# First layer norm and value projection of an embedding tower made once per table row

## Chip, cores and metric

The kernel runs on one core of a Trainium2 chip. The metric is the device time of one execution in microseconds (us); lower is better. Engines: PE (TensorE, matrix products), DVE (VectorE), ACT (ScalarE), POOL (GpSimd), and SP, which issues DMAs. They run side by side, each in its own fixed order, and wait for one another through semaphores.

## What is computed

4096 tokens (8 batches of 512) are indices into a codebook of 2048 rows. All arithmetic is float32. Cut to what matters:

```
h = gelu(codebook[x] @ W1 + b1) @ W2 + b2                 # 256 columns per token
n = layernorm(h)                                          # (h - mean) / sqrt(var + 1e-5)
x_tok, x_pos = n[:, :128], n[:, 128:]
q, k, v = rotate(x_pos @ Wq), x_pos @ Wk, x_tok @ Wv      # 16 heads of 64; k and v have 4 heads
att = q k^T / 8 + slope * (i - j), causal
e = exp(att - max(att));  att = e / (1 + sum(e))
h = h + (att @ v) @ Wo
h = h + (gelu(layernorm(h) @ U1 @ V1 + c1) @ U2) @ V2 + c2
```

h, n, x_tok, x_pos and v of a token hang on its codebook row alone, not on its place in the batch.

## The kernel before

It has two parts, one after the other, with a barrier between them.

**The table** (`token_table`). The first line of the network is made for all 2048 codebook rows, not per token, in NC = 4 chunks of 512 rows. A chunk has KH = 8 steps, so there are STEPS = 32. In step n PE makes `first_product(n)` (six products of 512 columns), ACT the gelu (`hid`, L243), DVE splits it into a high half `hid_hi` (L303) and a rest `hid_lo` (L305), and PE makes `second_product(n)` (twelve products of 256 columns) two steps later. Splitting into hi and lo and multiplying hi·hi, lo·hi and hi·lo is how the kernel keeps float32 accuracy all through. At the end of a chunk DVE adds b2 (`keep_rows`, L276, two halves) into `made`, and SP stores two halves of 256 rows of 1024 B to `token_table` in DRAM (L172). `keep_rows(i)` waits until the stores of chunk i-1 have landed. In its gaps DVE also makes the hi and lo halves of the other weights (`halves`, L314) and the rotated Wq (L317 to L341).

**The layer** (`layer`). POOL gathers a batch's 512 rows with four indirect DMAs of 128 rows (`gather`, L565) into `h`. Then 16 heads of each batch are 16 slots, s = 16 i + j for batch i and head j; each engine's order is written out by hand per slot. In slot s PE makes the scores of head s (L950, L951), DVE adds slope and mask and finds the extreme (`least_of`, L734), ACT exponentiates (L607), DVE inverts the sums (L741, L743), POOL multiplies (`normalize(s-1)`, L577). PE turns head s-2 (`turn`, ten transposes, L960), ACT moves it (L614), and PE makes the products with v for two heads in each even slot (`values`, L974). `first(s)` and `second(s)` say what else stands in slot s, and each engine walks both lists: q for the next pair of heads in even slots, k in slots 1, 5, 9 and 13; of the batch before, the output projection w in slots 3 to 6, the second norm transposed (y) in slot 10, u in 11, the gelu burst (f, g) in 12, d in 15.

The first norm and the values of batch i+1 stand inside batch i:

- POOL: `gather(i+1)` in slot 1, `root` (a power of -1/2, L571) in slot 3.
- DVE: `norm_front` (four BATCH_NORM_STATS2, L696, four aggregates, L700) after slot 3, `norm_back` (L708 to L723, writes `xn`) after slot 5.
- x in slot 7: four transposes of `xn` for the position half (in `first`), four for the token half (in `second`), L854. ACT takes the hi half of each (L634), DVE the lo half (L760).
- v in slots 10 and 11: twelve products with wv each batch, six per slot (L846), copied to `v_sb` by DVE (L765).

x, q, k, v and the second half of y share one PSUM bank (`a_bank`), each waiting until its forerunner has been read. For batch 0 the norm, x, k and q stand ahead of slot 0 (the opening), and v in slots 0 and 1.

## Time and profile before

| what | value |
|---|---|
| time, median of 3 runs | 1024.96 us (1024.83 to 1025.38) |
| the profiled execution's own time | 1025.75 us |
| its span, first to last instruction | 1023.9 us |
| PE busy | 883.8 us, 86% of the span |
| ACT busy | 700.5 us, 68% |
| DVE busy | 648.4 us, 63% |
| POOL busy | 630.8 us, 62% |
| mean granted PE clock | 0.963 of full |

The span is cut into stretches below. A slot's length is told from the start of its first exponential on ACT (the 128x512 one) to that of the next slot. Shares of busy time over the whole span mix stages that have different limits, so each stage is read by itself.

### The profile page before, as it was taken

The page shows a single profiled execution, that of the slowest core. Times are in us where ns is not written, and L with a number is a line of the kernel's source. Part 1 is how long each engine was busy: PE and PEld are TensorE (multiplying, and loading weights), DVE is VectorE, ACT ScalarE, POOL GpSimd, SP SyncE. Part 2 cuts the span into 40 slices and gives each one's busy share as a digit, 9 for nine tenths or more (in the row PEclk, how much of TensorE's full clock was granted, in tenths as well). Part 3 has the DMA queues.
Part 4 walks back from the last instruction along what each step waited for, and adds up shares of the span by engine and source line. Part 5 has one row for each costly group of instructions (what it writes and reads, how often), then busy time and mean ns, then how long its engine had stood idle before and what let it go on. Part 6 is the DMA issues. An engine that isn't in the chain of part 4 may idle for free.

```text
span 1023.9 us, 17066 instructions
## 1 busy us (share of the span) xinstructions
PE 883.8 (86%) x5616; PEld 681.8 (67%) x5616; DVE 648.4 (63%) x2000; ACT 700.5 (68%) x1564; POOL 630.8 (62%) x599
## 2 busy tenths in 40 slices
PE   6999369999888997899888979899889988998776
PEld 5898246768656775578657855686567765786563
DVE  4566377777837776476747784778457774667321
ACT  5332067996768777786788677867687777878713
POOL 6000249898747966586748774787569674868420
PEclk9999679999999999999999999999899999999997
DMA  9200100000000000000001000000000000000000
GB/s 259 49 21 21 42 21 1 2 12 12 1 1 21 22 1 1 12 30 1 1 1 43 1 1 1 27 16 1 1 21 22 1 1 1 22 1 1 1 21 21
DMA packets 13782, 18.89 MB, mean 18 GB/s; under 512 B 2320, under 2 KB 11696, under 8 KB 13696
## 3 DMA queue, kind: packets, MB, share of 16 engines
q1 hardware_dynamic: 11088, 10.62, 3.3%
q0 software_dynamic: 2608, 7.18, 2.7%
q8 instruction: 46, 0.75, 0.3%
q14 instruction: 40, 0.33, 0.1%
HBM read 11.51 MB, written 6.29 MB: 17 GB/s over the span
## 4 chain that ended last, share of the span: by engine, by line
PE 47%; DVE 15%; ACT 11%; issue 10%; POOL 5%; DMA 0%; DVEq 0%; POOLq 0%; ACTq 0%
PE ps L846 14%; PE ps L974 8%; PE ps L960 8%; ACT probs L607 6%; PE ps L950 5%; DVE probs L734 4%; PE ps L951 4%; PE ps L930 3%; POOL probs L577 3%; PE ps L924 2%; DVE q_both L751 2%; ACT turned_sb L614 2%; POOL h L565 1%; DVE xn L723 1%; PE ps L925 1%
## 5 line engine op out<-in xcount | busy, mean ns | idle before, releaser
L577 POOL TENSOR_SCALAR probs<-probs,recip 128x512 f32<-128x512 f32 (+3 forms) x512 | 546.2, 1084 | 220.7 <-DVE recip L743 220.3
L734 DVE CUSTOM_DVE_ANT_0 probs<-ps,causal,slope 128x512 f32<-128x512 f32 (+3 forms) x512 | 259.5, 547 | 62.4 <-PE ps L951 56.9
L607 ACT ACTIVATE probs<-probs,least 128x512 f32<-128x512 f32 (+3 forms) x512 | 282.0, 553 | 24.6 <-DVE least L734 20.1
L614 ACT ACTIVATE turned_sb<-ps 128x1280 f32<-128x1280 f32 x128 | 157.7, 1232 | 115.1 <-PE ps L960 114.9
L950 PE MATMUL ps<-k_hi,q_both 128*128 128x512 f32 (+3 forms) x512 | 185.5, 362 | 25.8 <-DVE least L734 23.0
L974 PE MATMUL ps<-turned_sb,v_sb 128*64 128x512 f32 (+3 forms) x1024 | 152.0, 438 | 23.1 <-ACT turned_sb L614 23.1
L960 PE MATMUL ps<-ident,probs 128*128 128x128 f32 x1280 | 167.1, 279 | 3.9 <-POOL probs L577 3.7
L951 PE MATMUL ps<-k_lo,q_both 128*128 128x512 f32 (+3 forms) x512 | 153.9, 326 | 0.0
L960 PEld LDWEIGHTS ps<-ident,probs 128*128 128x128 f32 x1280 | 148.8, 145 | 5.7 <-POOL probs L577 5.2
L974 PEld LDWEIGHTS ps<-turned_sb,v_sb 128*64 128x64 f32 x1024 | 73.1, 136 | 111.1 <-issue 96.5
L950 PEld LDWEIGHTS ps<-k_hi,q_both 128*128 128x128 f32 x512 | 98.0, 191 | 71.5 <-DVE least L734 47.7
L951 PEld LDWEIGHTS ps<-k_lo,q_both 128*128 128x128 f32 x512 | 98.6, 192 | 4.5
L607 ACT ACTIVATION_READ_ACCUMULATOR probs<-probs,least 128x1 f32 x512 | 96.2, 188 | 0.0
L624 ACT ACTIVATE q_both<-ps 64x512 fp32r<-64x512 f32 x128 | 75.4, 589 | 26.2 <-PE ps L846 24.7
L751 DVE TENSOR_TENSOR q_both<-ps,q_both 64x512 fp32r<-64x512 f32 x128 | 88.1, 689 | 7.8 <-ACT q_both L624 4.1
L846 PE MATMUL ps<-wo_hi,o_hi 128*128 128x256 f32 x224 | 62.6, 280 | 0.0
L846 PE MATMUL ps<-wo_lo,o_hi 128*128 128x256 f32 x224 | 62.6, 279 | 0.0
L846 PE MATMUL ps<-wo_hi,o_lo 128*128 128x256 f32 x224 | 62.5, 279 | 0.0
L243 ACT ACTIVATE hid<-ps,b_col 128x512 f32<-128x512 f32 x32 | 22.0, 688 | 57.0 <-PE ps L367 56.8
L792 DVE TENSOR_TENSOR o_lo<-ps,o_hi 128x512 fp32r<-128x512 f32 x64 | 44.2, 690 | 22.7 <-ACT o_hi L659 22.6
L783 DVE TENSOR_TENSOR y_lo<-ps,y_hi 128x512 fp32r<-128x512 f32 x8 | 5.5, 691 | 81.4 <-ACT y_hi L653 81.4
L580 POOL MEMSET minus_half<- 128x4 f32 x1 | 0.1, 101 | 90.5 <-POOLq L147 90.5
(163 smaller groups left out, 1515.1 us busy)
## 6 DMA issues: line engine op xcount, KB each, us to landing
out_dram<-h SPq DMA_DIRECT2D x7, 512.0 KB, 2.9
rows<-in_L_tok_codebook_dram SPq DMA_DIRECT2D x4, 512.0 KB, 8.5
token_table<-made SPq DMA_DIRECT2D x8, 256.0 KB, 2.3
w_f<-in_L_tok_W_dram SPq DMA_DIRECT2D x2, 512.0 KB, 6.4
w_f<-in_L_tok_W_dram SPq DMA_DIRECT2D x4, 256.0 KB, 8.4
wo_f<-in_L_attn_Wo_dram POOLq DMA_DIRECT2D x1, 1024.0 KB, 10.4
wq_f<-in_L_attn_Wq_dram POOLq DMA_DIRECT2D x1, 512.0 KB, 7.2
v_f<-in_L_ffn_V_dram POOLq DMA_DIRECT2D x2, 256.0 KB, 7.5
```

Of the source, the lines that this page charges most:

```text
L577: ins = pool.tensor_scalar(at, at, recip[:, s % P_RING, q:q + 1], None, ALU.mult)
L607: act.activation(at, at, ACT.Exp, bias=least[:, s % P_RING, q:q + 1], scale=-1.0, accum_out=sums[:, s % P_RING, q:q + 1]).then_inc(exped, 1)
L614: act.activation(turned_sb[:, s % 2, :], turn_ps, ACT.Copy).then_inc(moved, 1)
L624: act.activation(q_both[at, s % 4, :], a_of("q", n, 0)[at, :], ACT.Copy).then_inc(q_high, 1)
L734: dve.tensor_tensor_reduce(out=probs[:, s % P_RING, at], in0=bank(unit % 2)[:, UNIT_AT[q]:UNIT_AT[q] + P * (q + 1)], in1=causal[:, at], sc ...
L751: dve.tensor_tensor(q_both[to, s % 4, :], a_of("q", n, 0)[at, :], q_both[at, s % 4, :].bitcast(F32), ALU.subtract).then_inc(q_low, 1)
L792: dve.tensor_tensor(o_lo[:, p % O_RING, :], o_bank, o_hi[:, p % O_RING, :].bitcast(F32), ALU.subtract)\
L846: mm = pe.matmul(dst, w, x, start=n == 0, stop=n == len(parts) - 1)
L950: pe.matmul(dst, w, k_hi[:, slot, 0:P * (q + 1)], start=True, stop=False)
L951: mm = pe.matmul(dst, w, k_lo[:, slot, 0:P * (q + 1)], start=False, stop=True)
L960: mm = pe.transpose(turn_ps[:, K_AT[k] + P * (q - k):K_AT[k] + P * (q - k + 1)], probs[:, s % P_RING, Q_AT[q] + P * k:Q_AT[q] + P * (k + 1 ...
L974: mm = pe.matmul(o_bank[rows, P * k:T], v_sb[:, b % 2, k, n // REP, :], turned_sb[:, (s + e) % 2, K_AT[k]:K_AT[k] + T - P * k], start=k == ...
```

## The change

Each table row becomes ROW = 640 floats (2560 B): the embedding (256), the normed position half (128), and the values (256). The norm and the value projection are made in `token_table`, for 2048 rows instead of 4096 tokens. The layer gathers whole rows and takes the position half and v from them.

- In the table part, per chunk: DVE `norm_front` at step 2 of the next chunk and `norm_back` at step 4, POOL one power, PE `turn_tokens` (four transposes) at the end of step 5, ACT and DVE the hi and lo halves, PE `make_values` (twelve products of 256 columns) at the end of step 7, ACT two copies (`keep_values`). For the last chunk all of this stands behind step 31. The stores wait for `v_kept`, not `row_kept`.
- `hid_hi` is made by ACT, not DVE. The halves of the weights and the rotated Wq move by a few steps.
- In the layer: no first norm on DVE, no root for it on POOL, four transposes less and twelve products less per batch on PE, no `tok_hi`, `tok_lo`, no copy to `v_sb`.

```diff
-    table = nc.dram_tensor("token_table", (ROWS, DIM), F32, kind="Internal").ap()
+    table = nc.dram_tensor("token_table", (ROWS, ROW), F32, kind="Internal").ap()
...
-                    sp.wait_ge(row_kept, 2 * i + n + 1)
+                    sp.wait_ge(v_kept, 2 * i + n + 1)
...
-                                 made[:, 2 * n:2 * n + 2, :]).then_inc(stored, 16)
+                                 made[:, 2 * n:2 * n + 2, P:P + ROW]).then_inc(stored, 16)
...
+            def tok_highs(i):
+                act.wait_ge(tok_full, i + 1)
+                if i >= 1:
+                    act.wait_ge(v_full, 2 * i)
+                act.activation(tok_hi[:, :], ct_bank(0), ACT.Copy).then_inc(tok_high, 1)
+
+            def keep_values(i):
+                for n in range(2):
+                    act.wait_ge(v_full, 2 * i + n + 1)
+                    act.activation(made[:, 2 * n:2 * n + 2, 2 * P + DIM:P + ROW], ct_bank(1 - n).rearrange("p (t c) -> p t c", t=2),
+                                   ACT.Copy).then_inc(v_kept, 1)
...
+                act.activation(hid_hi[:, n % HID_RING, :], hid[:, n % 2, :], ACT.Copy).then_inc(hid_high, 1)
...
+                if i >= 1 and m == TURN_AT:
+                    tok_highs(i - 1)
+                if i >= 1 and m == VALUES_AT:
+                    keep_values(i - 1)
...
+            def norm_back(i):
+                dve.wait_ge(guess_done, i + 1)
...
+                if i >= 1:
+                    dve.wait_ge(tok_full, i)
+                for t in range(NT):
+                    halves_of = made[:, t, 0:2 * (P + DIM)].rearrange("p (a c) -> p a c", a=2)[:, :, 0:P]
+                    ins = dve.tensor_scalar(halves_of, made[:, t, P:P + DIM].rearrange("p (a c) -> p a c", a=2),
+                                            row_mv[:, t, 0:1], guess[:, t:t + 1], ALU.subtract, ALU.mult)
+                ins.then_inc(normed, 1)
...
-                dve.tensor_copy(hid_hi[:, n % HID_RING, :], hid[:, n % 2, :]).then_inc(hid_high, 1)
...
             keep_rows(NC - 1)
+            norm_front(NC - 1)
+            norm_back(NC - 1)
+            tok_lows(NC - 1)
...
+            def turn_tokens(i):
+                pe.wait_ge(normed, i + 1)
...
+            def make_values(i):
+                pe.wait_ge(tok_low, i + 1)
...
+                if KH <= n < STEPS and n % KH == TURN_AT:
+                    turn_tokens(n // KH - 1)
+                if KH <= n < STEPS and n % KH == VALUES_AT:
+                    make_values(n // KH - 1)
+            turn_tokens(NC - 1)
+            make_values(NC - 1)
...
-    if i + 1 < B and j == 7:
-        out.append(("x", i + 1, 1))
-    if i + 1 < B and j in (10, 11):
-        out.append(("v", i + 1, j - 10))
...
-                    pool.indirect_dma_start(out=h[:, b % 3, t, :], out_offset=None, in_=g["table"],
+                    pool.indirect_dma_start(out=token_rows[:, b % 3, t, :], out_offset=None, in_=g["table"],
...
-                if i + 1 < B and j == 3:
-                    root(("x", i + 1))
...
-                if i + 1 < B and j == 3:
-                    norm_front(("x", i + 1))
-                if i + 1 < B and j == 5:
-                    norm_back(("x", i + 1))
...
-                    pe.wait_ge(xn_done, norm_no["x", n])
-                    turn_rows(a_of("x", n, m), 1 - m).then_inc(x_full, 1)
...
+                    pe.wait_ge(rows_in, 16 * NT * (n + 1))
+                    turn_rows(a_of("x", n, m), pos[:, n % 3, :, :]).then_inc(x_full, 1)
```

PE's order in slot 10 of a batch, before: the scores' last unit, eight transposes of y (`xn`), six value products, the turn of head s-2.

```order
L951 MATMUL ps<-k_lo,q_both 128x256
L854 MATMUL ps<-ident,xn 128x128 x8
L846 MATMUL ps<-wv_hi,tok_hi 128x256
L846 MATMUL ps<-wv_hi,tok_lo 128x256
L846 MATMUL ps<-wv_lo,tok_hi 128x256
L846 MATMUL ps<-wv_hi,tok_hi 128x256
L846 MATMUL ps<-wv_hi,tok_lo 128x256
L846 MATMUL ps<-wv_lo,tok_hi 128x256
L960 MATMUL ps<-ident,probs 128x128 x10
L950 MATMUL ps<-k_hi,q_both 128x512
```

The same place after:

```order
L1016 MATMUL ps<-k_lo,q_both 128x256
L926 MATMUL ps<-ident,xn 128x128 x8
L1025 MATMUL ps<-ident,probs 128x128 x10
L1015 MATMUL ps<-k_hi,q_both 128x512
L1016 MATMUL ps<-k_lo,q_both 128x512
```

The six products are gone and the turn follows the transposes at once.

PE's order where the table ends and the layer begins, before: the last products of `second_product`, two branches, then the eight transposes of the opening.

```order
L382 MATMUL ps<-w_hi,hid_lo 128x256
L147 UNCONDITIONAL_BRANCH
L825 UNCONDITIONAL_BRANCH
L854 MATMUL ps<-ident,xn 128x128 x8
L846 MATMUL ps<-pos_hi,wk_hi 128x512
```

The same place after: four transposes of `made` and twelve value products follow the table's last product (the last five of the products, the two branches, four transposes of `token_rows` and k's products come behind these rows).

```order
L463 MATMUL ps<-w_hi,hid_lo 128x256
L473 MATMUL ps<-ident,made 128x128 x4
L482 MATMUL ps<-wv_hi,row_hi 128x256
L483 MATMUL ps<-wv_hi,row_lo 128x256
L484 MATMUL ps<-wv_lo,row_hi 128x256
L482 MATMUL ps<-wv_hi,row_hi 128x256
L483 MATMUL ps<-wv_hi,row_lo 128x256
L484 MATMUL ps<-wv_lo,row_hi 128x256
L482 MATMUL ps<-wv_hi,row_hi 128x256
```

These sixteen products and transposes moved ahead of the barrier.

DVE's order at the end of the table after; before, the two rows of `made` (L276) were its last there, and the norm (L696) stood behind the branch. `row_mv`, `row_var` and `row_guess` hold mean and variance, variance, and the power.

```order
L417 TENSOR_TENSOR wq_lo<-rot,wq_hi 128x1024
L316 TENSOR_TENSOR made<-ps,b_row 128x2x256 x2
L324 BN_STATS row_stats<-made 128x6 x4
L327 BN_AGGR row_mv<-row_stats 128x2 x4
L329 TENSOR_SCALAR row_var<-row_mv 128x4
L333 TENSOR_TENSOR row_tmp<-row_guess 128x4
L334 TENSOR_TENSOR row_tmp<-row_tmp,row_var 128x4
L335 TENSOR_SCALAR row_tmp<-row_tmp 128x4
L336 TENSOR_TENSOR row_guess<-row_guess,row_tmp 128x4
L341 TENSOR_SCALAR made<-made,row_mv,row_guess 128x2x128 x4
L347 TENSOR_TENSOR row_lo<-ps,row_hi 128x512
```

The norm of the last chunk now stands ahead of its stores, and the stores ahead of the barrier.

## Rows read from the trace of the kernel before

**Rows 1.** Busy time by stretch: us, then engines, PEclk, DMA share; table, then opening.

```profile
0.00:107.33 107.33, 97.51 (x608) 86.81 (x608) 62.11 (x113) 40.06 (x60) 15.88 (x30) 1.00 0.32 84
107.33:137.13 29.80, 9.32 (x28) 7.04 (x28) 11.72 (x34) 5.44 (x9) 5.35 (x6) 0.58 0.11 35
```

**Rows 2.** The same (PE, PEld, DVE, ACT, POOL), batch 2: slots 3, 4-6, 7, 8-9, 10-11, 12.

```profile
341.49:349.19 7.70, 7.63 (x53) 6.19 (x55) 5.40 (x23) 4.72 (x12) 7.70 (x9) 1.00 0.04 13
349.19:370.76 21.57, 21.53 (x166) 18.55 (x162) 15.17 (x49) 13.96 (x33) 15.89 (x15) 1.00 0.00 1
370.76:377.19 6.43, 5.54 (x37) 3.94 (x39) 4.77 (x20) 5.10 (x13) 2.99 (x4) 1.00 0.00 0
377.19:387.42 10.23, 9.06 (x60) 6.47 (x58) 9.86 (x33) 8.97 (x23) 9.38 (x10) 1.00 0.01 2
387.42:404.22 16.80, 13.24 (x81) 10.80 (x79) 11.26 (x33) 10.40 (x24) 12.21 (x11) 0.90 0.00 0
404.22:420.62 16.40, 14.45 (x78) 8.30 (x75) 5.18 (x16) 12.84 (x22) 4.39 (x5) 1.00 0.01 1
```

**Rows 3.** The same six stretches of slots in the last batch (batch 7).

```profile
887.06:894.49 7.43, 7.41 (x53) 6.17 (x55) 4.04 (x16) 4.72 (x12) 6.80 (x7) 1.00 0.01 2
894.49:915.49 21.00, 20.58 (x160) 17.88 (x156) 11.56 (x37) 13.45 (x32) 11.18 (x12) 1.00 0.00 1
915.49:920.12 4.63, 4.41 (x27) 3.35 (x29) 4.53 (x22) 4.58 (x11) 4.05 (x5) 1.00 0.00 0
920.12:930.04 9.92, 9.19 (x63) 6.79 (x60) 9.32 (x33) 9.07 (x22) 8.75 (x9) 1.00 0.01 2
930.04:944.66 14.62, 12.36 (x73) 9.69 (x71) 10.68 (x31) 10.41 (x25) 13.72 (x13) 0.88 0.00 1
944.66:960.25 15.59, 12.89 (x67) 7.07 (x64) 4.31 (x13) 12.24 (x21) 2.10 (x2) 1.00 0.00 1
```

**Rows 4.** Timeline of PE in slot 10 of batch 2: start, length, [idle before <-who ended it].

```profile
392.65 0.58 PE L846 MATMUL ps<-wv_hi,tok_hi 128*128 128x256 f32 x1 [2.31 <-DVE y_lo L776]
```

**Rows 5.** Busy time by stretch, batch 0: slots 3, 7, 9, 11.

```profile
149.57:159.50 9.93, 6.24 (x29) 4.64 (x31) 6.11 (x24) 4.70 (x12) 9.92 (x10) 0.66 0.05 13
...
174.10:180.00 5.90, 5.00 (x33) 3.55 (x34) 4.53 (x17) 5.19 (x14) 5.37 (x6) 1.00 0.02 4
184.83:189.35 4.52, 3.79 (x24) 2.53 (x24) 3.34 (x14) 4.47 (x12) 4.52 (x6) 1.00 0.00 0
...
194.40:199.72 5.32, 5.30 (x35) 4.06 (x37) 4.39 (x16) 4.71 (x11) 5.32 (x6) 1.00 0.01 3
```

**Rows 6.** The same: twelve products of `second_product` at full clock.

```profile
100.10:101.52 1.42, 1.42 (x13) 1.41 (x12) 0.46 (x2) 0.69 (x1) 0.00 (x0) 1.00 0.00 0
```

**Rows 7.** Group of the page: count, busy us, mean ns, idle before and its releaser.

```profile
L243 ACT ACTIVATE hid<-ps,b_col 128x512 f32<-128x512 f32 x32 | 22.0, 688 | 57.0 <-PE ps L367 56.8
```

**Rows 8.** Group of ACT's lines in the first 60 us, the same columns.

```profile
L237 ACT ACTIVATE w_hi<-w_f 128x512 fp32r<-128x512 f32 x4 | 2.5, 622 | 0.0
```

**Rows 9.** Timeline of DVE from the table's end to the opening.

```profile
106.73 1.40 DVE L276 TENSOR_TENSOR made<-ps,b_row 128x512 f32<-128x512 f32 x2 [1.74 <-PE ps L382]
118.66 1.41 DVE L696 BATCH_NORM_STATS2 stats<-h 128x6 f32<-128x256 f32 x4 [10.53 <-DMA h<-token_table,idx]
...
122.72 1.38 DVE L723 TENSOR_SCALAR xn<-h,mv,guess 128x256 f32<-128x256 f32 x4
```

**Rows 10.** Timeline of POOL in the same stretch: the last gather, the power.

```profile
115.75 1.01 POOL L565 DMA_INDIRECT h<-token_table,idx  x1 [0.30 <-issue]
120.83 1.05 POOL L571 TENSOR_TENSOR guess<-var,minus_half 128x4 f32<-128x4 f32 x1 [4.07 <-DVE var L703]
```

**Rows 11.** Timeline of PE in the same stretch: its first work of the layer.

```profile
124.15 1.97 PE L854 MATMUL ps<-ident,xn 128*128 128x128 f32 x8 [16.82 <-DVE xn L723]
```

**Rows 12.** DMA issues of the page: count, KB each, median us from issue to landing.

```profile
out_dram<-h SPq DMA_DIRECT2D x7, 512.0 KB, 2.9
...
token_table<-made SPq DMA_DIRECT2D x8, 256.0 KB, 2.3
```

More of the change, by code:

```diff
@@ L24 @@
 TRI = T * (NT + 1) // 2
+ROW = DIM + P + KVH * D
 MASKED = 1e30
@@ L198, in _ @@
                                         channel_multiplier=1))
+            pool.memset(power[:, :], -0.5).then_inc(half_set, 1)
             pool.wait_ge(w1_in[KD - 1], 16)
@@ L214, in _ @@
                            allow_slow_non_contiguous=True).then_inc(idx_in, 16)
+            pool.wait_ge(half_set, 1)
+            for i in range(NC):
+                pool.wait_ge(var_done, i + 1)
+                pool.tensor_tensor(guess[:, :], var[:, :], power[:, :], ALU.pow).then_inc(guess_done, 1)
         @block.scalar
@@ L512, in layer @@
     d_full, d_added = sem("d_full"), sem("d_added")
-    opening = [("x", 0, 0), ("x", 0, 1), ("k", 0, 0), ("q", 0, 0)]
-    home = {("x", 0, 0): c_bank, ("x", 0, 1): o_bank, ("q", 0, 0): bank(4)}
+    opening = [("x", 0, 0), ("k", 0, 0), ("q", 0, 0)]
+    home = {("x", 0, 0): c_bank, ("q", 0, 0): bank(4)}
     every = [("k", 0, 0)] + [use for s in range(SLOTS) for use in first(s) + second(s)]
@@ L538, in last_w @@
         return bank(RING_NO["W", B - 1, m] % 2)
-    norms = [("x", 0)]
-    for i in range(B + 1):
-        norms += [("x", i + 1)] * (i + 1 < B) + [("y", i - 1)] * (i >= 1)
+    norms = [("y", b) for b in range(B)]
     norm_no = {name: k + 1 for k, name in enumerate(norms)}
```

173 lines of the change are left out of this document (99 added, 74 removed).

## Prediction

> **What bounds the kernel now.** I read the busy time by stretch first, since the engines' shares over the whole span mix two different programs. In the table part PE is busy 97.51 of 107.33 us, and ACT and DVE have room [rows 1]; ACT's gelu waits 57.0 us in all, nearly all of it for PE [rows 7]. There every product added costs its own time. Then comes an opening of 29.80 us in which PE works 9.32 and its granted clock is 0.58 on average: a chain of DMA landings, DVE, POOL and ACT [rows 1]. In the layer the limit changes by slot. Slots 3 to 6 are PE's (21.53 of 21.57 us in three of them), slots 8 and 9 are DVE's (9.86 of 10.23), and in slots 10 and 11 PE works 13.24 of 16.80 with a wait of 2.31 us inside: the value products need the bank that the second half of y holds until DVE has made `y_lo` [rows 2, 4].
>
> The best witness for the layer is in the trace. Batch 7 has no batch after it, so its slots hold no first norm, no x and no v, but the same w, y, u and gelu burst of batch 6. Slots 3 to 12 take 79.13 us in batch 2 (the sum of rows 2; six batches, 1 to 6, are built like it) and 73.19 in batch 7 [rows 2, 3]. What the change leaves in and batch 7 lacks must be put back.
>
> **The layer, per steady batch.** Slot 3: 7.70 against 7.43, so 0.27 for `norm_front`, which stands ahead of the next slot's `least_of` on DVE. Slots 4 to 6: 21.57 against 21.00, but the position half of x stands at the head of slot 7, where its copy on ACT delays the exponential that closes slot 6. It stays, so I book 0. Slot 7: 6.43 against 4.63, a difference of 1.80. This is the token half: four transposes, a copy, DVE's rest. DVE still has to make `pos_lo` (0.70, as one of the two halves in rows 9) and is busy 4.53 of 4.63 in batch 7, so I take 1.6 rather than 1.8. Slots 8 and 9: 10.23 against 9.92, 0.31. Slots 10 and 11: 16.80 against 14.62, 2.18. This is twelve products (1.42 at full clock, [rows 6]) and the wait, less what comes next: in both batches a stretch at half clock falls here (PEclk 0.90 and 0.88). Slot 12: 16.40 against 15.59, but batch 7 lacks the k of slot 13, whose hi copy on ACT (about 0.6, [rows 8]) stands before the exponential that closes slot 12. I book 0. Sum 0.27 + 1.6 + 0.31 + 2.18 = 4.36, times six batches: 26.2 us. The bounds: 3.5 per batch if DVE eats the gain of slot 7, 5.94 if all of batch 7's lead is the change's; 21 to 36 us.
>
> Batch 0 has no batch before it. Slot 7 takes 5.90 against 4.52 in slot 9, a plain odd slot, and slot 11 takes 5.32 [rows 5]: 1.38 + 0.80 = 2.2. Slot 3 looks as if it would be freed, since 9.93 us pass there and DVE's first norm stands in it, but POOL is busy 9.92 of them [rows 5]: it is still behind from the gather. The turn waits for POOL's multiplication, which no edit touches. I book 0 (bounds 0 and -3). Batch 7 itself does not change. Layer: -28.4.
>
> **The table, inside.** Three chunks add to PE, which has no room: twelve products 1.42 [rows 6] and four transposes, a quarter of the 1.97 for eight at half clock [rows 11], 0.5; 5.7 in all. Two waits come with them. `turn_tokens` follows `second_product(n-2)` in step 5 and needs `normed`. From the end of `first_product` in step 4 PE has 1.42 + 1.42 + 1.42 = 4.3 us of its own work left (six products of 512 columns are as many columns as twelve of 256). The other side is gelu 0.69 [rows 7], the copy on ACT 0.62 [rows 8], `hid_lo` 0.70, then four tiny operations and four subtractions: from the power's end at 121.88 to 124.10 in the opening, about 2.2 [rows 9, 10]. With some 0.5 of hand-overs that is 4.7: PE waits 0.45, three times. And `hid_hi` on ACT takes 0.62 where the chain had DVE's quicker cast, which moves `keep_rows` and the first second product behind it by about 0.25, three times, and the start by 0.2. Sum 5.7 + 1.35 + 0.75 + 0.2 = +8.0. If the waits vanish it is 5.7; if each is twice as long, 10.
>
> **The last chunk's start.** `keep_rows(3)` waits for the stores of chunk 2, which are no longer issued four steps earlier but after `make_values(2)` in step 31. From the start of those products: half are done at 0.7, all at 1.4, the copies at 1.35 and 2.1. A store of 256 KB lands in 2.3, one of 512 KB in 2.9 [rows 12], so 0.6 for 256 KB of data; these are 640 KB each, 3.2 alone and 1.5 of it data. The first lands at 4.55, the second behind it at 6.05. PE has `second_product` 30 and 31 meanwhile, and `keep_rows` could have begun near 3.5 and ended at 5.0; now it ends at 6.05 + 1.40 = 7.45. +2.45, between 0 (if the stores are quick) and 3.5.
>
> **The tail and the opening.** What stood after the barrier stands before it now, and more. From the end of `keep_rows` (108.13): the norm 5.5, the same operations as from 118.66 to 124.10 [rows 9, 10]; PE has been idle and its clock was at half in this stretch (mean 0.58, [rows 1]), so four transposes take 1.0 and 0.15 to start [rows 11]; hi copy 0.65; rest 0.8; twelve products at half clock 2 x 1.42 + 0.2, about 3.1 [rows 6]; copy 0.6; store 3.25 (the second half's issue comes 1.45 after the first's and is again held by its data). That is 15.05, where 2.3 stood: +12.75. The bounds: 10.5 with full clock and a store of 2.3, and 14. In a sentence apart: the Trainium skill, in "DMA: Bandwidth & Descriptors", section "Anatomy of one DMA — SWDGE (gpsimd) path", gives 2.0 us plus bytes over 436 GB/s, fitted on the other issue path, so an estimate of 3.5 us for a 640 KB store and 2.6 for the old one, where the row has 2.3; the sum by it would be 0.3 more or the same, as the fixed part is set.
>
> Then the gather: its last issue ends at 116.76 and the data are there by 118.66 [rows 9, 10]. With 2.5 times the bytes I add 0.6 (bounds 0 and 1.5). After it PE transposes at once instead of waiting for the norm until 124.15: -5.5. Everything up to the first exponential (x, k, q, the table load of ACT) stays as it is. The v products in slots 0 and 1 go, but POOL's chain of multiply, gather, multiply holds those slots. Together -4.9, between -3.5 and -6.5.
>
> **The sum.** +8.0 + 2.45 + 12.75 - 4.9 = +18.3; the layer -28.4; net -10.1. The profiled execution has a span of 1023.9 and 1.85 us around it (1025.75), 0.8 above the median of 1024.96. So a span of 1013.8 and a median of 1024.96 - 10.1 = 1014.9 us.
>
> **Rivals.** *The layer gives all of batch 7's lead.* The wait of slot 10 goes and the gelu burst starts earlier, so 5.94 x 6 + 2.2 = 37.8 are saved against 18.3: 1005.5. For it: the slots are otherwise the same. Against it: k and the position half account for 1.2 of the 5.94.
>
> *The saved wait is only moved.* In slots 10 and 11 PE runs into POOL (busy 13.72 of 14.62 in batch 7, [rows 3]) and only PE's own work is saved: 1.9 per batch. Then 6 x 1.9 + 2.2 = 13.6 against 18.3: 1029.7, slower. It decides from the point where the multiplication of a head ends after the turn wants it, in slot 10. Against it: batch 7 has the same POOL work, and the gather's extra backlog is over by slot 5 (POOL 15.89 of 21.57 in slots 4 to 6, [rows 2]).
>
> *The gather's issue grows with the row.* An issue takes POOL 1.01 us for rows of 1024 B [rows 10]; no row shows a longer one. If it scales with bytes, 2.5 us each, four issues cost 6 more: once in the opening, and in slots 1 to 3 of seven batches, where POOL is full (7.70 of 7.70 in slot 3, [rows 2]). Up to 6 x 8 = 48 more: near 1063. Of this the Trainium skill says ("DMA: Bandwidth & Descriptors", the same section) that many descriptors can be written before the cost shows, and that one descriptor moves one contiguous run; by that rule the issue stays at 1.0 us, and no row here tests it.
>
> *The change does not do what it says.* The orders show the norm, the twelve products and four transposes gone from each batch, so I give it nothing.
>
> **Chances.** Forecast 0.67; all of batch 7's lead 0.12; wait only moved 0.07; gather issue 0.05; mixtures, such as a clock stretch that falls elsewhere (3 us), 0.09, half of them near no change. A difference under 0.2% (2 us) can't be told from none. Faster 0.83, same 0.06, slower 0.11. The range: the bounds of the table side (about +13 to +23) and of the layer (-23 to -36), not all at their ends together, 1004 to 1024.
>
> **What would show it.** Right: slots 7, 10 and 11 of batches 1 to 6 as long as batch 7's (7 a little over), each of them about 4.4 us shorter; the table's last second product ending near 115 (107.33 before); the first exponential near 155.4 (137.13 before). Wrong: a gather issue well over 1 us; PE waiting for POOL before the turn in slot 10; stores landing in over 4 us; an idle PE in slot 3 of batch 0 that is shorter than before.

## The result, and the profile after

The changed kernel takes 1009.01 us (median of four runs, 1007.94 to 1010.65) where the kernel before, run beside it, takes 1025.17 (1024.83 to 1027.34): a ratio of 0.9839, 95% interval 0.9819 to 0.9859, or 16.2 us saved. The forecast was 10.1 us saved, 1014.9 us, inside a range of 1004 to 1024. The profiled execution took 1009.6 us with a span of 1007.8.

I read the two ends first. These are the busy times by stretch of the changed kernel (us, then PE, PEld, DVE, ACT and POOL busy with their instructions, PEclk, DMA share, GB/s). The first is the table up to its last second product, the second the way from there to the first exponential.

```profile
0.00:114.48 114.48, 104.09 (x656) 92.56 (x656) 61.34 (x134) 65.55 (x101) 18.88 (x34) 1.00 0.34 95
114.48:155.31 40.83, 12.65 (x39) 9.53 (x39) 12.22 (x34) 6.64 (x10) 5.34 (x6) 0.62 0.23 77
```

Against [rows 1] the table is 7.15 us longer and the stretch behind it 11.03: the first exponential comes 18.18 us later. PE has 48 instructions more in the table (three chunks of twelve products and four transposes), and its busy time is up by 6.58 us. Its idle time went from 9.82 to 10.39 only, so PE hardly waits for the norm. The groups of PE's lines in the table say the same: the transposes (L473) have 0.3 us of idle time before them in all. The columns are count, busy us, mean ns, idle before and its releaser.

```profile
L461 PE MATMUL ps<-w_hi,hid_hi 128*128 128x256 f32 x128 | 36.5, 285 | 0.5 <-DVE made L316 0.3
...
L473 PE MATMUL ps<-ident,made 128*128 128x128 f32 x12 | 2.0, 286 | 0.3
```

Behind the table stands a chain of single steps. These are DVE's, PE's, ACT's and POOL's rows of its timeline (start, length, idle before and who ended it):

```profile
116.40 1.29 DVE L316 TENSOR_TENSOR made<-ps,b_row 128x512 f32<-128x512 f32 x2 [4.23 <-DMA token_table<-made]
117.72 1.41 DVE L324 BATCH_NORM_STATS2 row_stats<-made 128x6 f32<-128x256 f32 x4
...
121.90 1.38 DVE L341 TENSOR_SCALAR made<-made,row_mv,row_guess 128x256 f32<-128x256 f32 x4 [0.28 <-DVE row_guess L336]
```
```profile
123.33 1.12 PE L473 MATMUL ps<-ident,made 128*128 128x128 f32 x4 [8.86 <-DVE made L341]
125.86 0.58 PE L482 MATMUL ps<-wv_hi,row_hi 128*128 128x256 f32 x1 [1.41 <-DVE row_lo L347]
...
142.26 1.12 PE L926 MATMUL ps<-ident,token_rows 128*128 128x128 f32 x4 [13.48 <-DMA token_rows<-token_table,idx]
```
```profile
128.82 0.60 ACT L252 ACTIVATE made<-ps 128x512 f32<-128x512 f32 x1 [0.68 <-PE ps L484]
```
```profile
134.24 1.17 POOL L662 DMA_INDIRECT token_rows<-token_table,idx  x1 [0.74 <-issue]
...
138.37 1.01 POOL L662 DMA_INDIRECT token_rows<-token_table,idx  x1 [0.30 <-issue]
```

`keep_rows` of the last chunk waits 4.23 us for the stores of the chunk before. The norm runs to 123.28, PE answers with its clock at half (its four transposes take 1.12 us), the last store is issued at 129.4 and has landed by 132.9. The gather's issues are as short as before, 1.01 to 1.17 us for rows of 2560 bytes against 1.01 for 1024 [rows 10]; the last one ends at 139.38 and PE starts 2.88 us after it. The page's DMA issues (count, KB each, median us to landing) stand beside [rows 12]:

```profile
token_table<-made SPq DMA_DIRECT2D x8, 640.0 KB, 3.3
out_dram<-token_rows SPq DMA_DIRECT2D x7, 512.0 KB, 2.9
```

Then the layer. From the first exponential to the end of the span it takes 852.5 us where it took 886.8: 34.3 less. The stretches of batch 2 that answer to [rows 2], slots 3, 4 to 6, 7, 8 and 9, 10 and 11, 12:

```profile
353.59:361.27 7.68, 7.62 (x53) 6.18 (x55) 4.34 (x16) 4.71 (x11) 7.68 (x9) 1.00 0.15 45
361.27:382.85 21.58, 21.58 (x168) 18.81 (x165) 12.15 (x39) 13.96 (x34) 14.87 (x14) 1.00 0.00 1
382.85:387.38 4.53, 3.81 (x25) 2.64 (x25) 4.43 (x19) 4.48 (x13) 3.33 (x5) 1.00 0.00 2
387.38:397.27 9.89, 9.16 (x62) 6.79 (x60) 9.51 (x33) 9.09 (x22) 9.04 (x9) 1.00 0.01 2
397.27:410.23 12.96, 10.83 (x73) 8.35 (x71) 10.53 (x31) 10.30 (x25) 12.24 (x11) 1.00 0.00 1
410.23:426.63 16.40, 14.46 (x78) 8.31 (x75) 5.27 (x16) 12.84 (x22) 4.40 (x5) 1.00 0.00 0
```

Slot 7 gave 1.90 us, slots 8 and 9 0.34, slots 10 and 11 3.84. Slots 3, 4 to 6 and 12 gave nothing. But slots 10 and 11 are not the same in every batch now. Here they are in batch 1 of the changed kernel:

```profile
292.55:307.09 14.54, 12.42 (x73) 9.63 (x71) 10.66 (x31) 10.41 (x25) 13.04 (x12) 0.88 0.00 1
```

Batches 1, 3 and 5 look like this row, with TensorE's clock at half (1.2 GHz) for part of slot 11, and batches 4, 6 and 7 like the row of batch 2 above, at full clock. The kernel before had such a stretch in batches 1 to 5 and in batch 7. So two things differ: work that is gone, and half-clock stretches that are gone. The experiments take them apart.

### The profile page after: what moved, and what is told of

The parts are those of the page before. It is cut to its first block, busy times and chain, and to the rows that moved or that the text cites. A ratio compares the mean times of both kernels' runs of the same rounds, so it can differ in the third digit from the quotient of the medians.

```text
span 1007.8 us, 16846 instructions
## 1 busy us (share of the span) xinstructions
PE 871.6 (86%) x5552; PEld 672.6 (67%) x5552; DVE 608.9 (60%) x1880; ACT 722.9 (72%) x1600; POOL 626.9 (62%) x596
## 4 chain that ended last, share of the span: by engine, by line
PE 50%; DVE 15%; ACT 12%; issue 8%; POOL 1%; DMA 0%; DVEq 0%; ACTq 0%; POOLq 0%
PE ps L918 15%; PE ps L1039 10%; PE ps L1025 8%; ACT probs L701 6%; PE ps L1015 5%; DVE probs L818 5%; PE ps L1016 4%; PE ps L995 3%; ACT turned_sb L708 2%; PE ps L989 2%; DVE q_both L835 2%; DVE xn L807 1%; DVE recip L825 1%; PE ps L990 1%; DVE o_lo L870 1%
## 5 line engine op out<-in xcount | busy, mean ns | idle before, releaser
L1039 PE MATMUL ps<-turned_sb,token_rows 128*64 128x512 f32 (+3 forms) x1024 | 152.0, 438 | 29.8 <-ACT turned_sb L708 29.8
L1025 PE MATMUL ps<-ident,probs 128*128 128x128 f32 x1280 | 164.7, 277 | 3.8 <-POOL probs L674 3.6
L1039 PEld LDWEIGHTS ps<-turned_sb,token_rows 128*64 128x64 f32 x1024 | 74.8, 136 | 116.8 <-issue 99.7
L1025 PEld LDWEIGHTS ps<-ident,probs 128*128 128x128 f32 x1280 | 146.6, 143 | 6.8 <-POOL probs L674 5.2
L232 POOL TENSOR_TENSOR row_guess<-row_var,row_power 128x4 f32<-128x4 f32 x4 | 4.1, 1025 | 97.2 <-DVE row_var L329 97.2
L825 DVE TENSOR_SCALAR recip<-sums 128x4 f32<-128x4 f32 x128 | 33.9, 265 | 33.8 <-ACT probs L701 33.5
```

Source lines behind the costliest of these rows:

```text
L1025: mm = pe.transpose(turn_ps[:, K_AT[k] + P * (q - k):K_AT[k] + P * (q - k + 1)], probs[:, s % P_RING, Q_AT[q] + P * k:Q_AT[q] + P * (k + 1 ...
L1039: mm = pe.matmul(o_bank[rows, P * k:T], v_rows[:, b % 3, k, n // REP * D:(n // REP + 1) * D], turned_sb[:, (s + e) % 2, K_AT[k]:K_AT[k] + ...
```

## Experiments

Unless another base is named, each run is the changed kernel with one edit. All but the last two runs are a single execution. Four executions of the changed kernel lie 2.7 us apart, so a smaller difference in a run's time shows nothing by itself, and what I read from such a run is the length of its slots. The table part varies too. In the eight runs that leave it alone its last second product ends between 114.28 and 115.37. In the seven of them that also have the changed layer's opening, the first exponential comes between 155.3 and 156.2; the profiled run of the changed kernel stands at the low end (114.48 and 155.31).

**The token half of x, put back.** Four transposes, a copy and a subtraction come back in slot 7.

```
+    if i + 1 < B and j == 7:
+        out.append(("t", i + 1, 0))
...
+                if kind == "t":
+                    turn_rows(a_bank, pos[:, n % 3, :, :]).then_inc(t_full, 1)
```

> The changed kernel with one thing put back in the layer as extra work whose result nobody reads: in slot 7 of batches 0 to 6 a second set of four transposes, its copy on ACT and its subtraction on DVE (before, they made the value half of the normed rows). Theory A (the layer's gain in slot 7 is this work): slot 7 of the steady batches goes back from 4.53 to about 6.4 us, slots 8 and 9 from 9.90 to about 10.2, slots 10 and 11 stay, so a steady batch is about 2.0 to 2.2 us longer and the kernel about 14 us slower, near 1023. Rival B (slot 7 shortened because the first norm no longer runs on DVE in slots 3 to 5 and the engines come to slot 7 less late): slot 7 stays within 0.3 us of 4.53 and the time within 3 us of the changed kernel's 1009.

It took 1027.73 us. Slots 7, then 8 and 9 of batch 2:

```profile
388.57:395.00 6.43, 5.55 (x37) 3.92 (x39) 4.76 (x20) 5.09 (x14) 2.99 (x4) 1.00 0.00 1
395.00:405.23 10.23, 9.08 (x60) 6.49 (x58) 9.86 (x33) 8.97 (x22) 9.38 (x10) 1.00 0.01 2
```

These are the lengths of [rows 2] to the hundredth, so 2.24 us a batch hang on this work: theory A on the mechanism, and B is out. The time is 5 us over theory A's. A mean batch is 2.82 longer, not 2.0 to 2.2, since there are five stretches at half clock where the changed kernel has three (four in slot 11, one in slot 15 of batch 1). Batch 0 is 1.1 longer, and the first exponential comes 0.5 later.

**The value products, put back.** Twelve products and two DVE copies in slots 10 and 11.

```
+    if i + 1 < B and j in (10, 11):
+        out.append(("v", i + 1, j - 10))
```

> The changed kernel with the twelve value products and their two DVE copies put back in slots 10 and 11 of batches 0 to 6, as extra work whose result nobody reads (they multiply the transposed position half by the first block of Wo, of the same shapes). Theory A (the gain of slots 10 and 11 is these products, and the half-clock stretch that only every second batch now has comes back in every batch with them): slots 10 and 11 together go from 12.96 or 14.54 to about 16.8 us in every steady batch, a batch is about 3.0 us longer in the mean, the kernel 20 us slower, near 1029. Rival B (the half clock comes and goes with the batch length, not with this work): slots 10 and 11 grow by 2.2 us in the batches that have a half-clock stretch now and the stretches stay in every second batch, so the kernel is 15 us slower, near 1024.

It took 1029.15 us, and a mean batch is 2.81 longer (106.75 against 103.94). Slots 10 and 11 of batches 1, 3, 4 and 5:

```profile
294.69:311.21 16.52, 14.04 (x85) 11.21 (x83) 11.33 (x33) 10.51 (x24) 12.20 (x11) 0.90 0.01 1
...
508.61:524.40 15.79, 12.54 (x85) 9.85 (x83) 11.26 (x33) 10.41 (x25) 12.22 (x11) 1.00 0.01 2
614.55:629.97 15.42, 12.51 (x85) 9.83 (x83) 11.24 (x33) 10.40 (x24) 12.20 (x11) 1.00 0.01 2
720.15:737.83 17.68, 15.20 (x85) 12.38 (x83) 11.35 (x33) 10.52 (x25) 12.21 (x11) 0.81 0.00 1
```

The time is theory A's, but its condition "in every batch" does not hold: batches 3 and 4 run at full clock. The kernel before has one such batch too. These are its slots 10 and 11 in batch 5, which has the most half clock, and in batch 6, which has none:

```profile
715.28:733.08 17.80, 14.47 (x79) 11.92 (x77) 11.41 (x33) 10.51 (x25) 12.33 (x11) 0.81 0.00 1
825.52:840.95 15.43, 11.85 (x81) 9.43 (x79) 11.24 (x33) 10.41 (x25) 12.20 (x11) 1.00 0.00 0
```

Compared at like clock the products are worth 15.43 - 12.96 = 2.47 us at full clock and 16.80 - 14.54 = 2.26 with one stretch at half. Batch 4 of this run gives the same at full clock, 15.42 - 12.96. Of the 2.47, PE's busy time makes 1.02 (11.85 against 10.83) and its idle time 1.45 (3.58 against 2.13). The rest of the difference between two batches is the clock.

**The first norm, put back.** DVE's statistics, four small steps and four subtractions, and POOL's power.

```
+                if i + 1 < B and j == 3:
+                    more_front(i + 1)
+                if i + 1 < B and j == 5:
+                    more_back(i + 1)
```

> The changed kernel with the first norm put back in the layer for batches 1 to 7 (statistics in slot 3, the power on POOL, the normed rows in slot 5) as extra work whose result nobody reads. Theory A (this work lay in idle time of DVE and never set the pace): slots 3 to 6 stay at 7.69, 7.63, 6.61, 7.33 within 0.1 us each, and the kernel within 2 us of 1009. Rival B (it cost what the prediction booked in slot 3, 0.27 us a batch, or more in slots 4 to 6 with their full DVE): 0.3 to 1.0 us a batch, 2 to 7 us for the kernel.

It took 1011.03 us; the mean steady batch is 103.94 us, as without it. Slot 3 and slots 4 to 6 of batch 2:

```profile
355.10:362.77 7.67, 7.62 (x53) 6.18 (x55) 5.38 (x23) 4.71 (x11) 7.67 (x9) 1.00 0.16 50
362.77:384.34 21.57, 21.57 (x168) 18.79 (x165) 15.17 (x49) 13.96 (x34) 15.91 (x15) 1.00 0.00 1
```

DVE has 4 us more to do (5.38 and 15.17 busy against 4.34 and 12.15) and no slot of the steady batches grows. The time is 2.0 us over 1009, at the edge between the two theories, but none of it lies in those slots: batch 0 is 0.6 longer and the first exponential comes 0.85 later. Theory A for the steady batches. The three parts put back make 2.82 + 2.81 + 0.00 = 5.63 us a batch, where the change gave 109.22 - 103.94 = 5.28.

**The gather, moved.** What makes slot 3 longer than in batch 7, if not the norm?

```
-                if i + 1 < B and j == 1:
+                if i + 1 < B and j == 4:
                     gather(i + 1)
```

> The changed kernel with the next batch's gather issued on POOL at the start of slot 4 instead of slot 1. Theory A (the 0.27 us by which slot 3 is longer in the steady batches than in batch 7, which has no gather, is the gather's delay of POOL's products and not the first norm's): slot 2 falls from 4.72 to 4.33 and slot 3 from 7.69 to 7.43 us, and in batch 0 the 10.8 us of slot 3 fall to about 7; slot 4 is filled by PE and POOL has room, so it grows by under 0.4 us: the kernel is 2 to 6 us faster, 1003 to 1007. Rival B (the gather's four issues cost the same wherever they stand, since POOL is behind by 4 us after them in any slot): slots 2 and 3 fall as above, slots 4 to 6 grow by as much or more, time within 1 us of 1009 or up to 5 us slower.

It took 999.3 us, 9.7 below the median of the changed kernel and more than the 2 to 6 of theory A. Slot 3 of batch 0, then slots 2, 3 and 4 to 6 of batch 2:

```profile
168.12:172.73 4.61, 4.39 (x27) 3.35 (x29) 3.40 (x15) 4.56 (x12) 4.61 (x5) 1.00 0.00 0
...
343.41:347.74 4.33, 3.92 (x32) 3.13 (x28) 3.44 (x10) 4.13 (x10) 3.39 (x4) 1.00 0.00 0
347.74:355.17 7.43, 7.41 (x53) 6.16 (x55) 4.04 (x16) 4.72 (x11) 6.82 (x7) 1.00 0.01 2
355.17:376.75 21.58, 21.58 (x168) 18.80 (x165) 12.27 (x39) 13.96 (x34) 15.97 (x16) 1.00 0.21 62
```

The 0.27 us of slot 3 and the 0.39 of slot 2 were the gather's. Slots 4 to 6 take the gather in for nothing (21.58 as before), since PE fills them anyway. In batch 0 slot 3 falls from 10.82 to 4.61, and the batch from 79.5 to 75.8; slots 6 and 7 give back part of it (6.49 and 5.26 against 4.91 and 4.52). Half clock in slot 11 is down to one batch. In the two traces batches 0 to 6 are 10.4 us shorter together: 3.7 in batch 0, 3.6 in slots 2 and 3, and 3.2 from two half-clock stretches fewer in slot 11, which this edit was not meant to touch.

**The table under the old layer.** The table part of the changed kernel, and the layer of before, which reads only the embedding from the long rows (a cut of the edit):

```
+    if i + 1 < B and j == 7:
+        out.append(("x", i + 1, 1))
+    if i + 1 < B and j in (10, 11):
+        out.append(("v", i + 1, j - 10))
...
-    h, pos, v_rows = token_rows[:, :, :, 0:DIM], token_rows[:, :, :, DIM:DIM + P], token_rows[:, :, :, DIM + P:ROW]
+    h = token_rows[:, :, :, 0:DIM]
```

> The changed kernel's table (rows of 640 values, with normed half and values, hid_hi on ACT) under the layer of before, which gathers whole 2560-byte rows, reads the embedding alone and makes its own first norm and values, so that the table's additions are paid and bring nothing. Theory A (cost and gain add up: the table's side is paid once, in full, ahead of the layer): first exponential at about 137.1 + 18.2 + 5.5 = 160.8 us, batches as before (109.3), time 1025 + 23.7 = 1049 us. Rival B (part of the table's cost is made good later, as DMA and POOL work that the layer of before waits for anyway in batch 0): under 1040 us. If the longer gather delays POOL further in slots 1 to 3, the steady batches are longer than 109.3 by the difference.

It took 1052.88 us beside 1025.92 for the kernel before: +27.0 where 23.7 was expected. The first exponential comes at 160.65, 23.5 later than before, as booked. The layer took 2.7 of the rest: batch 0 is 0.9 longer and the six steady batches 1.5 together (109.47 against 109.22 in the mean). Another 0.8 lies around the span. Theory A, 3 us off. Nothing of the table's cost comes back later.

**Two buffers of made rows.** The wait of 4.23 us, removed by what makes it wait.

```
-    made = sb("made", [P, NT, P + ROW])
+    made2 = sb("made", [P, 2, NT, P + ROW])
...
-                    if i >= 1:
-                        dve.wait_ge(stored, 16 * 2 * i)
+                    if i >= 2:
+                        dve.wait_ge(stored if i % 2 else stored_even, 16 * 2 * (i // 2))
```

> The changed kernel with two buffers of made rows, so that the rows of chunk 3 need not wait for the stores of chunk 2 (one more wait on PE, for the values of the chunk before, is met by then). Theory A (the wait of 4.2 us ahead of the last rows is the whole delay between the last product and the last rows): the last rows are kept 0.8 us after the last product instead of 3.2, everything behind moves forward by 2.4, the kernel is 2.4 us faster, near 1006.6. Rival B (the stores of chunk 3 then meet those of chunk 2, or the norm waits for something else): gain under 1 us.

It took 1006.22 us. DVE's row of the last kept rows waits for PE now, and the first exponential comes at 152.6 instead of 155.3 to 156.2: theory A, at least 2.7 us for 2.4.

```profile
113.56 1.40 DVE L318 TENSOR_TENSOR made<-ps,b_row 128x512 f32<-128x512 f32 x2 [1.71 <-PE ps L465]
```

**Idle products for the clock.** In the changed kernel PE is idle for 1.94 us near the end of slot 10 (batch 1 here, 1.94 to 1.97 in all seven):

```profile
299.50 0.38 PE L1015 MATMUL ps<-k_hi,q_both 128*128 128x256 f32 x1 [1.94 <-DVE least L818]
```

The edit puts seven products that nobody reads into this gap.

```
+                if s // HEADS >= 1 and s % HEADS == 9 + LAG:
+                    pe.wait_ge(y_low, KD * (s // HEADS - 1) + 1)
+                    for _ in range(7):
+                        pe.matmul(c_bank, g["wq_hi"][:, 0:P], g["wq_hi"][:, 0:512], start=True, stop=True,
+                                  skip_group_check=True)
```

> The changed kernel with seven idle products of 128x512 (result unread, into the bank that y's first half has left) on PE at the start of slot 11 of batches 1 to 8, where PE otherwise waits 1.95 us for DVE's minimum before the second half clock begins. Theory A (the 3.4 us at half clock in slot 11 of some batches, 1.6 us each, follow that idle time): no half-clock stretch at slot 11 in any batch, slot 11 at 6.0 to 6.2 us in all, slot 10 unchanged within 0.2, the kernel 3 to 5 us faster, 1004 to 1007. Rival B (the half clock comes from something else, such as the load of the slots before): the stretches stay in two to four batches, slot 11 at 7.6 there, and the time stays at 1008 to 1011 us.

It took 1004.28 us. PE's timeline in the gap of batch 1, then slots 10 and 11 by busy time:

```profile
297.46 1.83 PE L1055 MATMUL ps<-wq_hi 128*128 128x512 f32 x7
299.61 0.39 PE L1015 MATMUL ps<-k_hi,q_both 128*128 128x256 f32 x1 [0.31 <-DVE least L818]
```
```profile
292.62:299.58 6.96, 6.51 (x45) 5.07 (x41) 6.28 (x16) 5.10 (x12) 6.62 (x6) 1.00 0.00 1
299.58:305.60 6.02, 6.00 (x35) 4.45 (x37) 4.26 (x16) 5.20 (x13) 5.64 (x6) 1.00 0.01 3
```

Slot 11 takes 6.02 us in all seven batches, where the changed kernel has 7.61 to 7.65 in three. So a stretch at half clock costs 1.6 us here. That it hangs on the idle time before it rests on more than this run. Six runs leave the gap at 1.94 to 1.97 us (the changed kernel, x1_back, norm_back, gather_slot4, made_twice, hid_hi_on_dve), and slot 11 has the stretch in 17 of their 42 batches. Of the 28 batches with a shorter gap (0.31 here, 1.22 in c2_late, three_moves and three_moves_warm), none has it. Theory A, with one limit: the gap is followed by half clock in fewer than half of the batches, and which ones these are stays open. Slot 10 itself is no shorter for the products.

**POOL's addition of c2, later.** What makes PE idle there? It waits for DVE's minimum (`least`), which stands behind these rows of DVE. Next to them is POOL's row of the same time, all in slot 10 of batch 1 of the changed kernel:

```profile
296.44 1.29 DVE L854 TENSOR_TENSOR y_lo<-ps,y_hi 128x512 fp32r<-128x512 f32 x2 [0.55 <-ACT y_hi L731]
297.65 0.89 DVE L825 TENSOR_SCALAR recip<-sums 128x4 f32<-128x4 f32 x1
```
```profile
296.13 2.37 POOL L691 TENSOR_TENSOR token_rows<-token_rows,c_row 128x1024 f32<-128x1024 f32 x1
```

DVE's addition on 4 numbers per partition (`recip`) takes 0.89 us and ends at 298.54; POOL's ends at 298.50.

```
-                if i >= 1 and j == 8 + LAG:
+                if i >= 1 and j == 10 + LAG:
                     b = i - 1
```

> The changed kernel with POOL's addition of c2 to the batch's rows (2.37 us) moved from the start of slot 10 to the start of slot 12. Theory A (the 0.89 us of DVE's 128x4 addition at 297.65, 0.47 elsewhere, ends with POOL's addition: DVE is held by it, the slot's first minimum comes late and PE idles 1.95 us): that addition takes under 0.5 us, slot 10 falls from 6.94 to about 6.3 us in every batch and the slots at half clock may go, since PE idles less: 4 to 9 us faster, 1000 to 1005. Rival B (slot 10 is set by the chain through y, its copies and the minimum, with or without POOL): slot 10 within 0.2 us of 6.94, time 1008 to 1011 us.

It took 999.66 us. The same DVE row, PE's row behind the gap, and slot 10 of batch 1:

```profile
298.11 0.16 DVE L825 TENSOR_SCALAR recip<-sums 128x4 f32<-128x4 f32 x1
```
```profile
299.24 0.39 PE L1015 MATMUL ps<-k_hi,q_both 128*128 128x256 f32 x1 [1.22 <-DVE least L818]
```
```profile
293.02:299.22 6.20, 4.83 (x38) 3.91 (x34) 5.52 (x16) 5.09 (x12) 4.26 (x5) 1.00 0.00 1
```

0.16 us for 0.89, slot 10 down by 0.73 in every batch, and no stretch at half clock in slot 11 of any: PE idles 1.22 us there instead of 1.94. Theory A; the time is 0.3 us under its range of 1000 to 1005. The Trainium skill says in "SBUF — State Buffer", section "SBUF: two separate sides", that DVE in some modes and GpSimd share one pair of ports as an exclusive lock for a whole instruction, so that the second fully blocks. The two ends 0.04 us apart agree, as does `y_lo`, which reads PSUM and takes 1.29 us for two both beside the addition and without it.

**The same move in the kernel before.**

> The kernel before with the addition of c2 moved from slot 10 to slot 12 and nothing else. It asks whether the twelve value products cost 3 us in slots 10 and 11 by themselves, or because POOL's addition makes DVE late there. Theory A (the products by themselves): slots 10 and 11 fall by 0.7 us or less from 16.8 us and keep their half clock, the time falls by 0 to 5 us from 1025. Rival B (with POOL out of the way the slot absorbs the products, so that the change's gain in slot 10 was in part a matter of the addition): slots 10 and 11 fall by 2 us or more, the time by 14 us or more.

```
-                if i >= 1 and j == 8 + LAG:
+                if i >= 1 and j == 10 + LAG:
                     b = i - 1
```

It took 1026.19 us (the kernel before took 1025.74 to 1028.99 beside it). Slots 10 and 11, batches 2 and 7:

```profile
388.61:405.63 17.02, 13.44 (x81) 11.01 (x79) 11.24 (x33) 10.42 (x25) 9.90 (x10) 0.90 0.00 0
931.85:944.08 12.23, 10.70 (x73) 8.27 (x71) 9.79 (x31) 10.30 (x24) 9.91 (x10) 1.00 0.01 1
```

The time can't be told from that of the kernel before. With the value products in the slots the move brings nothing (17.02 against 16.80 in [rows 2]). In batch 7, which has none, it takes 14.62 [rows 3] down to 12.23: 0.73 in slot 10, and 1.64 in slot 11, where the half clock is gone. So POOL's addition sets the pace only where the products are gone. Theory A. The trace of the kernel before shows it already, in DVE's `recip` of slot 10 in batches 2 and 7:

```profile
394.94 0.16 DVE L741 TENSOR_SCALAR recip<-sums 128x4 f32<-128x4 f32 x1
...
935.14 0.90 DVE L741 TENSOR_SCALAR recip<-sums 128x4 f32<-128x4 f32 x1
```
```profile
933.63 2.38 POOL L597 TENSOR_TENSOR h<-h,c_row 128x1024 f32<-128x1024 f32 x1
```

In batch 7 it ends with POOL's addition (936.04 and 936.01). In batch 2, as in all batches with the products, it starts after the addition has ended and takes 0.16. So the change uncovers this wait, and part of the gain is lost to it. With the addition out of the way the products are worth 15.45 (batch 6 of this run) - 12.22 (c2_late) = 3.23 us at full clock instead of 2.47.

**The rounded hidden values on DVE again.**

```
-                act.activation(hid_hi[:, n % HID_RING, :], hid[:, n % 2, :], ACT.Copy).then_inc(hid_high, 1)
...
+                dve.tensor_copy(hid_hi[:, n % HID_RING, :], hid[:, n % 2, :]).then_inc(hid_high, 1)
```

> The changed kernel with the rounded hidden values (hid_hi) made on DVE again, as before, with the norm, the turned rows and the value copies where the change put them. The prediction booked 0.75 us for ACT making them (three delays of 0.25 where the kept rows come late). Theory A (that price is right): the last second product ends 0.5 to 1.0 us earlier than 114.48, the time near 1008.5. Rival B (DVE, which has the norm's work now, becomes the late engine in chunks 1 to 3 without ACT's help): the last second product ends 1 to 4 us later, the time 1010 to 1013.

It took 1008.58 us, which can't be told from the changed kernel. The last second product ends at 113.33, 1.15 us earlier than in the changed kernel's profile and 0.95 to 2.0 earlier than in the eight runs with the same table. That is the upper end of theory A or more; B would have had it later, and DVE is not the late engine. It is busy 74.20 us of 113.33:

```profile
0.00:113.33 113.33, 102.73 (x656) 91.92 (x656) 74.20 (x166) 45.44 (x69) 19.55 (x34) 1.00 0.34 96
```

**Three moves together**: the gather in slot 4, the addition of c2 in slot 12, two buffers of made rows.

> The changed kernel with three of the edits together: the gather in slot 4, the addition of c2 in slot 12, two buffers of made rows. Theory A (they lie in different places and add up): 1009.6 less 2.4 for the table, 3.9 in batch 0 and 0.65 in each of six batches for the gather, 0.73 in each of seven for c2, and three or four stretches at half clock of 1.6 each, so 987 to 990 us, a ratio of 0.964 to before. Rival B (the moved gather and addition meet at POOL or PE in slots 4 and 12 once slot 10 is short, or half clock appears in another slot): 993 us or more.

991.24 us (990.74 to 992.7), a ratio of 0.9645 to before (0.9629 to 0.9661): theory A, 1.2 us above its range. Slots 4 and 5 of batches 2 and 5 show where that went:

```profile
353.11:367.75 14.64, 14.51 (x110) 12.21 (x108) 8.18 (x27) 9.21 (x23) 12.73 (x13) 1.00 0.31 91
...
659.44:673.67 14.23, 14.23 (x110) 12.24 (x108) 8.26 (x27) 9.32 (x22) 12.73 (x13) 1.00 0.32 93
```

Five of six batches take 0.3 to 1.1 us more there than with the gather moved alone (14.24). In batch 2 the 0.40 us arise at one place. PE's load of the weights for the last two products of scores (`k_hi`, 128x256) comes after 0.57 us of idle time, put down to DVE's minimum, and after 0.13 with the gather moved alone. DVE's rows just before stand at the same distance from the slot's start in both runs. The reason stays open.

**And warm.** On top of these, 30 idle products on PE and one small exponential on ACT while the layer waits for its first rows.

```
+            for _ in range(30):
+                pe.matmul(bank(0), g["wq_hi"][:, 0:P], g["wq_hi"][:, 0:512], start=True, stop=True, skip_group_check=True)
...
+            act.activation(early[:, :], minus_half[:, :], ACT.Exp)
```

> The kernel of the run three_moves with two idle pieces of work while the layer waits for its first gather: 30 products of 128x512 on PE (result unread, into bank 0) and one 128x4 exponential on ACT. Theory A (the opening's products run at half clock because PE idled 13.5 us, and the exponentials' table, 1.28 us, is loaded only behind the copies): the products from 142 to 153 us take 0.40 instead of 0.63 us, the table's load leaves the chain, the first exponential comes 3 to 4 us earlier, and batch 0 loses part of its two half-clock stretches: 982 to 986 us. Rival B (the chain there is set by the copies, or PE's clock falls again at once): under 1.5 us of gain.

989.11 us (988.36 to 989.97), ratio 0.9629 (0.9612 to 0.9646), the fastest kernel of this study. Beside three_moves the medians are 2.1 us apart, and the time is 3 us over theory A's 982 to 986, though the opening did what theory A says:

```profile
130.89 9.41 PE L1052 MATMUL ps<-wq_hi 128*128 128x512 f32 x30 [4.75 <-POOL minus_half L681]
140.14 0.60 PE L932 MATMUL ps<-ident,token_rows 128*128 128x128 f32 x4
```

The transposes take 0.60 instead of 1.12, ACT loads its table at 130.7 instead of 151.8, and the first exponential comes at 148.6 instead of 153.1, 4.5 us earlier. Of this 1.3 is the table's load, which took 1.28 us right ahead of that exponential, and 3.2 come from PE, whose products and transposes run faster. The layer takes as long as in three_moves (837.9 against 837.8): the steady batches are 0.13 us longer (102.34 against 102.21), why, I did not find out, and batch 0 is 0.6 shorter. So the two profiled executions are 4.3 us apart, but they are the slowest of four of three_moves and the fastest of four here. Why the medians are only 2.1 apart the traces can't say.

## Why the prediction was right, and where it was off

**The table, inside: +7.15 for +8.0.** The total held, the split did not. I booked 5.7 for PE's work and 2.1 for two kinds of waiting. The work is 6.58: four transposes take 0.66 and twelve products 1.6 by themselves, where I had 0.5 and 1.42. The idle time grew by 0.57. Of the 0.45 at each `turn_tokens` 0.3 in all is left. The chain over gelu, copy and norm is quicker than the 4.7 us I gave it: in chunk 1 it runs from 48.64, the gelu's start, to 52.88, the norm's end, 4.24 us, because the hand-overs that I put at 0.5 hardly show. `hid_hi` on ACT was a real term: 1.15 measured between two single executions, 0.95 at the least, for the 0.75 (and 0.2 at the start) that I had. The table's own end varies by 1.1 us between executions, so the total of 7.15 is no better known than that.

**The last chunk's start: +2.4 for +2.45.** The last rows were kept 3.2 us after the last product, 0.8 before. The two-buffer run took the wait away, and its first exponential came 2.7 earlier.

**Tail and opening: 15.24 us from the kept rows to the landing, for 15.05; +1.0 for the gather's landing, for +0.6.** Reading the norm's length from the opening of before, and doubling PE's lengths because it had been idle, was right to 0.2 us. A 640 KB store lands in 3.3, where I had 3.2 from two sizes of [rows 12]. By the Trainium skill's formula for the other issue path ("DMA: Bandwidth & Descriptors", "Anatomy of one DMA — SWDGE (gpsimd) path") the estimate was 3.5. What the prediction took from the same page on descriptors, that the issue would not grow with the row, agrees with the trace: the issue stays at 1.0, and that rival would have been 48 us. (One of the two statements, that a descriptor moves one contiguous run, stands in another section of that page, "Why a DMA increments its semaphore by 16 and not by 1".) The first exponential came 18.2 us later; 18.3 was forecast. That close an agreement is luck in part: the table came out 0.85 low and the tail and the gather 0.6 high, and the first exponential varies by 0.9 between executions.

**The layer: -34.3 for -28.4.** This is the whole error of the forecast. By steps: slot 7 gave 1.90 for 1.6, since DVE did not take its share back, 1.8 us over six batches. Slots 8 and 9 gave 0.34 for 0.31. Slot 3 gave 0.00 for 0.27: the step "0.27 for `norm_front`" is the one that failed in its mechanism. Batch 7 lacks the gather as well as the norm, and I charged the difference to the wrong one. The norm put back costs nothing in the steady batches (7.67 in slot 3), and the gather moved takes slot 3 to batch 7's 7.43. Slots 10 and 11 gave 17.8 us over six batches for 13.1: there the step that was mis-sized is "in both batches a stretch at half clock falls here". As the price of the products the pair was fair, 2.26 to 2.47 at like clock for 2.18. But it kept a stretch in every batch, and the changed kernel has it in three. Of the 17.8, six times 2.47 = 14.8 are the products and 3.0 the clock; batch 7, where the change removes no work in these slots, gave 14.62 - 12.96 = 1.66 more by its clock alone. Batch 0 gave 1.36 of 2.2: slot 7 its 1.38, slot 11 its part, and POOL's backlog in slot 3 stayed as booked and grew, 10.82 for 9.93. In all: slot 7 +1.8, products +1.7, clock +3.0 and +1.7, slots 8 and 9 +0.2, slot 3 -1.6, batch 0 -0.8. These are the 6 us between forecast and trace.

**The rivals.** "All of batch 7's lead" has its number in the neighbourhood (a steady batch is 5.28 shorter, not 5.94) but not its mechanism: slots 3, 4 to 6 and 12 did not move. "The saved wait is only moved" did not happen as it was told, since PE's idle time in slots 10 and 11 fell by 1.45 us at full clock. But there is something in it. POOL is busy 12.24 of 12.96 us there, and its addition of c2 holds DVE, whose minimum PE now awaits for 1.94 us. The rival looked at POOL's multiplication and the turn; it was POOL's addition and DVE.

So the range held and the forecast was 6 us too high. The largest part of that, 4.7 us, is clock that came back. The prediction had such a stretch only among its mixtures, at 3 us and without a sign. Its size is luck in part: the other runs that leave the gap alone have one to four of these stretches in slot 11 where the changed kernel has three, and at 1.6 us each the term would be 3.2 us larger or 1.6 smaller with theirs. The rest is small errors of both signs.

## What to carry to other kernels

A batch that lacks the work in question is a good witness, but list everything it lacks before charging a slot's difference to one part: here the gather, not the norm. When work goes away from a slot, look at who is left waiting there and for what. An operation that was covered, like POOL's addition, then sets the slot. Moving it by two slots brought 9.4 us (one execution against a median) where the whole change brought 16.2. And when a half-clock stretch shows in a row, book it as a term of its own with a sign of its own, because removing work can remove it or bring it on.

## What the runs showed of the hardware

- The same schedule meets the half clock in some batches and not in others: in batches 1, 3 and 5 of the changed kernel, in one of seven with the gather moved. Each stretch costs 1.6 us there. Over six runs an idle time of PE of 1.94 to 1.97 us was followed by one in 17 of 42 cases; 1.22 us, or 0.31 after the idle products, was followed by one in none of 28.
- A 128x4 operation of DVE took 0.89 us instead of 0.16 while a 2.37 us addition of POOL, with both its inputs in SBUF, was running, and ended with it; with the addition moved it took 0.16. DVE's two subtractions from PSUM took 1.29 us with and without the addition beside them.
- An indirect gather of 128 rows took POOL 1.01 us to issue at 1024 bytes a row, and 1.01 to 1.17 at 2560. In batch 0, where POOL has no slack, moving the four issues from slot 1 to slot 4 was worth 3.7 us (79.5 against 75.8).
- ACT's load of the table for the exponential took 1.28 us. It stood between the last copy and the first exponential, and one small exponential made while ACT waited anyway took it off the chain.
